# Eleven products of constant tiles per group on TensorE in the second layer of a graph network kernel

## The chip, the cores and the metric

One core of one Trainium2 chip. The metric is the device time of one execution in microseconds (us), the median of repeated runs.

## What is computed

Two graph layers over 3125 nodes with 256 features and 50000 edges, sorted by destination, each followed by a residual and a layer norm:

```python
x = layernorm(x + L0(x, edge_attr, src, dst, ...))   # edge MLP, gated, mean over the senders
x = layernorm(x + L1(x, [src, dst], edge_weight, W, a_src, a_dst))

def L1(x, edge_index, edge_weight, W, a_src, a_dst): # 4 heads of 64
    h = einsum('ni,hio->hno', x, W)
    e = (h@a_src)[:, src] + (h@a_dst)[:, dst]
    e = where(e >= 0, e, 0.2 * e) * edge_weight
    e_exp = exp(e - max(e))
    alpha = e_exp / (segment_sum(e_exp, dst)[:, dst] + 1e-10)
    return segment_sum(h[:, src] * alpha, dst)       # per head, heads side by side
```

The change is in the second layer, L1, in the part that scores and sums the edges.

## The kernel before

The 50000 edges lie in 391 blocks of 128, and 4 blocks make a group: 98 groups (NG). The first layer runs group by group to about 1640 us, then node products write the table HT (features and source score of each node), and from about 1700 us the second layer runs over the same 98 groups. The engines have instruction streams of their own, written out by hand and tied by semaphores. In the second layer's loop:

- POOL gathers the rows of HT by source index into Hg, one indirect DMA for each block (`gather_h_rows`, L1345). Hg is a ring of 12 groups (HGR): the gathers of group g wait for `s_xb`, which tells that DVE has used group g-12.
- DVE, in iteration i: `weighted_rows(i)` (xb, L911), `window_rows(i+1)` (in_window, L859), `edge_scores(i+1)` (L873 to L895, ends with `diag`, a diagonal matrix of the group's maxima), `one_hot(i+3)` (hot, L849), `carry_window(i-1)` (L928, L937, reads the sums of group i-1), `running_maximum(i+1)` (L902 reads `top_g` from the bank of `spread_maxima`, L906 makes neg_m).
- ACT, for group g: three exponentials of the scores with the running maximum (L1853, L1860, L1862); they wait for neg_m, and xb waits for them.
- PE, in iteration i: `destination_scores(i+2)` (L1601, 12 products of 4 columns into bank PAD), `spread_maxima(i+1)` (L1610, ones x diag, waits for diag), `window_sums(i)` (L1620, waits for in_window and xb).
- SP stores each group's sums and loads the destination remainders (`rem`) for two groups at a time.

So every group goes round one loop: top_g, neg_m (DVE), exponentials (ACT), xb, in_window, scores, diag (DVE), spread_maxima (PE), top_g of the next group (DVE). Scores of group g are in the first 16 columns of bank `PAD[g % 2]`, which is bank 0 or 1; columns 64 to 511 of the two banks are not read in this stage. `in_tile` (128 x 98 x 25, bf16) is a table that DVE makes once, before the loop; the constant "outside" of the semaphore `s_dc` is counted some instructions after it.

Of the kernel before, what the change touches and what calls it, by code (L numbers as in the profile page):

```python
# [6 lines left out]
P = 128  # L7
# [10 lines left out]
def build_program(nc, xT, x, src_cols, dst_cols, src_row, dst_row, eT, w_cols,  # L18
# [11 lines left out]
    NG = -(-NB // BLOCKS_PER_GROUP)  # L30
# [35 lines left out]
    def rows_of_block(b):  # L66
        return min(P, E - b * P)

    def blocks_of_group(g):
        return range(g * BLOCKS_PER_GROUP, min((g + 1) * BLOCKS_PER_GROUP, NB))  # L70
# [26 lines left out]
    with ctx:  # L97
        def sb(name, shape, dt=f32, scope=ctx):
            return scope.enter_context(nc.sbuf_tensor(name, shape, dt))

        def sem(name):
            return ctx.enter_context(nc.semaphore(name))
# [125 lines left out]
        outside = sb("outside", [1, 1], i32, sc)  # L228
        in_tile = sb("in_tile", [P, NG, NT], bf16, sc)
# [88 lines left out]
        PAD, PTOP, PS = bank[0:2], bank[2:4], bank[4:8]  # L318
# [10 lines left out]
        s_dc = sem("s_dc")  # L329
# [177 lines left out]
        def if_outside(eng):  # L507

            eng.wait_ge(s_dc, DC["outside"])
            return eng.If(eng.value_load(outside[0:1, 0:1], min_val=0, max_val=1))  # L510
# [4 lines left out]
        DC, B2 = {}, {}  # L515
# [895 lines left out]
        def _(pe):  # L1411
# [180 lines left out]
            def destination_scores(g):  # L1592

                pe.wait_ge(s_hot, g + 1)
                pe.wait_ge(s_adw, g // ADC + 1)
                if g >= 2:
                    pe.wait_ge(s_sc, 3 * (g - 2) + 1)
                for j, b in enumerate(blocks_of_group(g)):
                    n = rows_of_block(b)
                    for part in range(3):  # L1600
                        last = pe.matmul(PAD[g % 2][0:n, j * HEADS:(j + 1) * HEADS], hot[:, g % HOTR, j * P:j * P + n],  # L1601
                                         ad_p[:, part, g, :], start=part == 0, stop=part == 2)
                last.then_inc(s_ad, 1)

            def spread_maxima(g):

                pe.wait_ge(s_topc, 2 * g + 2)
                if g >= 2:
                    pe.wait_ge(s_mg, g - 1)
                pe.matmul(PTOP[g % 2][:, 0:P], ones[:, :], diag[:, g % 2, :], start=True, stop=True).then_inc(s_sp, 1)  # L1610

            def window_sums(g):

                pe.wait_ge(s_win, g + 1)
                pe.wait_ge(s_xb, g + 1)
                if g >= 4:
                    pe.wait_ge(s_carry, g - 3)
                for j, b in enumerate(blocks_of_group(g)):
                    n = rows_of_block(b)
                    last = pe.matmul(PS[g % 4][:, 0:BW], in_window[0:n, g % XBR, j, :], xb[0:n, g % XBR, j, :],  # L1620
                                     start=j == 0, stop=b == blocks_of_group(g)[-1])
                last.then_inc(s_S, 1)

            pe.wait_ge(s_hc, NT)
            pe.wait_ge(s_x1c, NT)
            for i in range(-2, NG):
                if i + 2 < NG:
                    destination_scores(i + 2)
                if 0 <= i + 1 < NG:
                    spread_maxima(i + 1)  # L1630
                if i >= 0:
                    window_sums(i)

            with if_outside(pe):
                pe.wait_ge(s_b2, B2["ones"])
# [21 lines left out]
                for t in range(NT):  # L1657
# [6 lines left out]
                    for k in range(DK):  # L1664
                        last = pe.matmul(bank[1][0:n, 0:OUT + 2 * HEADS], x1T_u[:, k, 0:n], Wc[:, k, :],
                                         start=k == 0, stop=k == DK - 1)
                    last.then_inc(s_vpe, 1)
                for b in range(NB):
                    n = rows_of_block(b)
                    pe.wait_ge(s_b2, B2[("weighed", b)])  # L1670
                    if b >= 1:
                        pe.wait_ge(s_vact, VACT1 + 1 + b)
                    pe.matmul(bank[0][0:n, 0:BW], in_window[0:n, 0, 0, 0:n], xb[0:n, 0, 0, :],
                              start=True, stop=True).then_inc(s_vpe, 1)
# [278 lines left out]
```

## Time and profile before

| | us |
|---|---|
| median of 3 runs | 2475.72 (2471.28 to 2481.22) |
| the profiled execution | 2482.71 |
| its span, first to last instruction | 2480.9 |
| second layer's group loop, first to last top_g | 1716.3 to 2412.2 |

The page gives for each engine the busy time and, in 40 slices of 62 us, its busy share and the clock granted to TensorE. The timeline lists instructions in order of time, equal ones merged with their count, and in brackets how long the engine had been idle and what released it. PE is the matmul side of TensorE, PEld its weight loads. A matmul's end is modelled, its start is recorded.

### The profile page before, as it was taken

Reading aid. Unit: us, or ns where it says so; the run is one execution under the profiler, and the core shown is the slowest. Engines: PE = TensorE matmul, PEld = TensorE weight load, DVE = VectorE, ACT = ScalarE, POOL = GpSimd, SP = SyncE. Lnnn points to the kernel's source line nnn. Section 1 sums busy time; section 2 is a strip of 40 time slices with the busy share of each in tenths; the row PEclk is TensorE's granted clock in tenths of the full one; section 3 lists DMA queues with packets and bytes.
Section 4 is the critical chain, followed back from the end, with each engine's and each line's share of the span. In section 5 each row is a group of like instructions: output and inputs, shape, how many; then the busy total and the mean of one; then the engine's idle time right before and its main releaser. Section 6 shows DMA issues by size and latency. Waiting matters only on the chain.

```text
span 2480.9 us, 41573 instructions
## 1 busy us (share of the span) xinstructions
PE 2001.8 (81%) x12990; PEld 1768.5 (71%) x12990; DVE 1594.5 (64%) x4240; ACT 1414.6 (57%) x2926; POOL 1467.6 (59%) x1204
## 2 busy tenths in 40 slices
PE   7699999999999999999999999944355555556560
PEld 6589999999999999899999999933244444444450
DVE  6466666666666666666666666652376656566575
ACT  4288888888888888888888888833011111111112
POOL 0327777877676677777777777424555565555503
PEclk9799999999999999999999999967566676766785
DMA  7678877777777777777777777564344444444413
GB/s 279 195 208 183 198 165 165 169 168 167 161 159 159 158 158 158 158 158 161 157 162 157 161 157 161 116 177 118 96 109 115 114 121 113 123 107 114 118 49 107
DMA packets 236177, 370.90 MB, mean 150 GB/s; under 512 B 35853, under 2 KB 168935, under 8 KB 235949
## 3 DMA queue, kind: packets, MB, share of 16 engines
q0 software_dynamic: 101232, 188.20, 38.4%
q1 hardware_dynamic: 134717, 179.94, 24.5%
q8 instruction: 108, 1.77, 0.3%
q14 instruction: 120, 0.98, 0.1%
HBM read 270.57 MB, written 97.45 MB: 148 GB/s over the span
## 4 chain that ended last, share of the span: by engine, by line
PE 56%; issue 17%; DVE 11%; another core or an unknown queue 5%; DMA 5%; ACT 4%; POOL 1%; SPq 0%; DVEq 0%; ACTq 0%; POOLq 0%
PE bank L1414 12%; PE bank L1415 12%; PE bank L1416 12%; PE bank L1466 4%; PE bank L1457 4%; PE bank L1483 3%; DMA accA<-ystage,to_a 2%; DVE in_window L859 2%; PE bank L1507 2%; PE bank L1518 2%; PE bank L1508 2%; PE bank L1519 2%; PE bank L1581 1%; ACT drop L1853 1%
## 5 line engine op out<-in xcount | busy, mean ns | idle before, releaser
L1310 POOL DMA_INDIRECT accA<-ystage,to_a x391 | 647.9, 1657 | 228.9 <-issue 107.7
L1316 POOL DMA_INDIRECT GA<-TA,src_c x391 | 424.0, 1084 | 334.4 <-issue 93.6
L1345 POOL DMA_INDIRECT Hg<-HT,src_c x391 | 371.5, 950 | 350.7 <-DVE xb L911 187.9
L1853 ACT ACTIVATE drop<-neg_m 128x1 f32<-128x1 f32 x98 | 28.9, 295 | 627.5 <-DVE neg_m L906 359.8
L1414 PE MATMUL bank<-h1h,W1h 128*128 128x512 f32 x882 | 349.6, 396 | 8.4 <-DVE h1l L531 7.6
L1416 PE MATMUL bank<-h1h,W1l 128*128 128x512 f32 x882 | 348.6, 395 | 0.0
L1415 PE MATMUL bank<-h1l,W1h 128*128 128x512 f32 x882 | 347.5, 394 | 0.0
L531 DVE TENSOR_TENSOR h2l<-h2f,h2h 128x512 fp32r<-128x512 f32 (+1 forms) x294 | 202.9, 690 | 203.2 <-ACT h2l L1689 72.2
L1610 PE MATMUL bank<-diag,ones 128*128 128x128 f32 x196 | 69.4, 452 | 304.5 <-DVE diag L895 249.9
L1620 PE MATMUL bank<-xb,in_window 128*128 128x260 f32 (+1 forms) x782 | 305.4, 561 | 0.0
L531 DVE TENSOR_TENSOR h1l<-h1f,h1h 128x512 fp32r<-128x512 f32 x294 | 195.1, 691 | 145.1 <-ACT h1h L1689 127.7
L1610 PEld LDWEIGHTS bank<-diag,ones 128*128 128x128 f32 x196 | 43.4, 276 | 313.5 <-DVE diag L895 255.5
L1620 PEld LDWEIGHTS bank<-xb,in_window 128*128 128x128 f32 (+1 forms) x782 | 220.2, 295 | 45.9
L1689 ACT ACTIVATE mh<-mf 128x512 fp32r<-128x512 f32 x196 | 124.0, 633 | 205.8 <-DVE mf L671 191.4
L1721 ACT ACTIVATE h1f<-bank 128x512 f32<-128x512 f32 (+1 forms) x392 | 206.9, 584 | 44.3 <-PE bank L1466 35.9
L1415 PE MATMUL bank<-W2l,h2h 128*128 128x256 f32 (+1 forms) x782 | 220.9, 282 | 0.0
L1414 PE MATMUL bank<-W2h,h2h 128*128 128x256 f32 (+1 forms) x782 | 219.8, 281 | 0.4 <-DVE mf L671 0.4
L1416 PE MATMUL bank<-W2h,h2l 128*128 128x256 f32 (+1 forms) x782 | 219.4, 281 | 0.0
L1746 ACT ACTIVATE h2f<-bank,b1c 128x512 f32<-128x512 f32 x294 | 201.9, 687 | 7.1 <-issue 1.7
L1414 PEld LDWEIGHTS bank<-h1h,W1h 128*128 128x128 f32 x882 | 166.7, 189 | 43.3 <-DVE h1l L531 9.8
L1416 PEld LDWEIGHTS bank<-h1h,W1l 128*128 128x128 f32 x882 | 166.1, 188 | 39.4
L1689 ACT ACTIVATE h2h<-h2f 128x512 fp32r<-128x512 f32 x294 | 185.5, 631 | 9.3
(208 smaller groups left out, 5189.7 us busy)
## 6 DMA issues: line engine op xcount, KB each, us to landing
TW<-TB SPq DMA_DIRECT2D x196, 203.0 KB
ef<-in_eT SPq DMA_DIRECT2D x97, 256.0 KB
bcast_i<-in_src_row SPq DMA_DIRECT2D x97, 256.0 KB
HB<-hist SPq DMA_DIRECT2D x98, 130.0 KB
rel<-RL SPq DMA_DIRECT2D x97, 128.0 KB
rem<-RD SPq DMA_DIRECT2D x48, 256.0 KB
TB<-stB SPq DMA_DIRECT2D x24, 406.0 KB, 3.3
accA<-zeros SPq DMA_DIRECT2D x4, 1677.0 KB, 13.5
```

Of the source, the lines that this page charges most:

```text
L531: return dve.tensor_tensor(o, full, hi.bitcast(f32), ALU.subtract)
L1310: return pool.indirect_dma_start(out=table, out_offset=bass.IndirectOffsetOnAxis(ap=rows, axis=0), in_=sums, in_offset=None, compute_op=AL ...
L1316: pool.indirect_dma_start(out=GA[0:n, b % (GAR * BLOCKS_PER_GROUP), :].bitcast(f32), out_offset=None, in_=TA, in_offset=bass.IndirectOffse ...
L1345: pool.indirect_dma_start(out=Hg[0:n, slot, :], out_offset=None, in_=HT, in_offset=bass.IndirectOffsetOnAxis(ap=src_c[0:n, b:b + 1], axis= ...
L1414: pe.matmul(o, lh, rh, start=first, stop=False)
L1415: pe.matmul(o, lh, rl, start=False, stop=False)
L1416: return pe.matmul(o, ll, rh, start=False, stop=last)
L1610: pe.matmul(PTOP[g % 2][:, 0:P], ones[:, :], diag[:, g % 2, :], start=True, stop=True).then_inc(s_sp, 1)
L1620: last = pe.matmul(PS[g % 4][:, 0:BW], in_window[0:n, g % XBR, j, :], xb[0:n, g % XBR, j, :], start=j == 0, stop=b == blocks_of_group(g)[-1])
L1689: return act.activation(o, i, ACT.Copy)
L1721: act.activation(h1f[0:k1(c), c, 0:n], PT[u % 2][0:k1(c), 0:n], ACT.Tanh).then_inc(s_tanh1, 1)
L1746: act.activation(h2f[:, m, 0:n], PL1[u % 2][:, 0:n], ACT.Tanh, bias=b1c[:, m:m + 1]).then_inc(s_tanh2, 1)
```

## The change

After the products of the sums of group i, PE issues eleven bf16 products: the first 128 columns of `in_tile` are the stationary tile, the next 448 the moving one, and the output goes to columns 64 to 511 of bank `PAD[(i + 1) % 2]`. Nothing reads the output, and no semaphore is raised. They are issued for i = 0 to 94, 95 x 11 = 1045 products. A wait of PE for "outside" stands ahead of the loop, so that `in_tile` is there.

```diff
+            def keep_running(g):
+
+                flat = in_tile[:, :, :].rearrange("p g t -> p (g t)")
+                for _ in range(11):
+                    pe.matmul(PAD[(g + 1) % 2][:, 64:512], flat[:, 0:P], flat[:, P:P + 448], start=True, stop=True)
+
             pe.wait_ge(s_hc, NT)
             pe.wait_ge(s_x1c, NT)
+            pe.wait_ge(s_dc, DC["outside"])
             for i in range(-2, NG):
                 if i + 2 < NG:
                     destination_scores(i + 2)
@@
                 if i >= 0:
                     window_sums(i)
+                if i + 3 < NG:
+                    keep_running(i)
```

## Rows read from the trace of the kernel before

**Rows 1.** The page's slices: PE's busy tenths, and its granted clock in tenths

```profile
PE   7699999999999999999999999944355555556560
...
PEclk9799999999999999999999999967566676766785
```

**Rows 2.** Stretches of the loop: busy time (count) of each engine, clock, DMA

```profile
1800.00:2350.00 550.00, 318.18 (x1759) 250.31 (x1760) 340.91 (x999) 54.60 (x237) 303.37 (x320) 0.68 0.46 116
2360.00:2400.00 40.00, 26.82 (x190) 21.53 (x189) 30.84 (x96) 5.53 (x24) 0.00 (x0) 0.82 0.15 46
```

**Rows 3.** Waits, 1800 to 2400 us: who waited for whom, total, times, longest

```profile
POOL Hg L1345 <- DVE xb L911: 173.3, 62, 7.7
DVE top_g L902 <- remote: 115.8, 36, 4.1
...
DVE top_g L902 <- issue: 7.7, 3, 3.3
```

**Rows 4.** Timeline, a group late in the loop, POOL's gathers over, clock high

```profile
2361.25 0.29 DVE L895 TENSOR_SCALAR diag<-ident,top_c 128x128 f32<-128x128 f32 x1
...
2361.59 0.49 PE L1610 MATMUL bank<-diag,ones 128*128 128x128 f32 x2 [0.48 <-DVE diag L895]
...
2362.48 0.28 DVE L902 TENSOR_REDUCE top_g<-bank 128x1 f32<-128x128 f32 x1
...
2363.67 0.44 PE L1601 MATMUL bank<-ad_p,hot 128*128 128x4 bf16 x12
...
2366.61 0.49 PE L1610 MATMUL bank<-diag,ones 128*128 128x128 f32 x2 [2.50 <-DVE diag L895]
...
2367.50 0.28 DVE L902 TENSOR_REDUCE top_g<-bank 128x1 f32<-128x128 f32 x1
```

**Rows 5.** Timeline of PE, the group before it, clock low

```profile
2356.57 0.79 PE L1610 MATMUL bank<-diag,ones 128*128 128x128 f32 x2 [6.40 <-DVE diag L895]
2357.15 3.67 PE L1620 MATMUL bank<-xb,in_window 128*128 128x260 f32 x8
2360.62 0.49 PE L1601 MATMUL bank<-ad_p,hot 128*128 128x4 bf16 x12
```

**Rows 6.** Timeline of a group with a stall, clock low in it

```profile
2029.24 0.80 PE L1610 MATMUL bank<-diag,ones 128*128 128x128 f32 x2 [0.46 <-issue]
2029.83 3.56 PE L1620 MATMUL bank<-xb,in_window 128*128 128x260 f32 x8
2031.58 0.95 POOL L1345 DMA_INDIRECT Hg<-HT,src_c  x1 [0.30 <-issue]
2034.25 0.29 DVE L902 TENSOR_REDUCE top_g<-bank 128x1 f32<-128x128 f32 x1 [4.04 <-remote]
2036.98 0.94 POOL L1345 DMA_INDIRECT Hg<-HT,src_c  x1 [4.45 <-DVE xb L911]
2038.39 0.79 PE L1610 MATMUL bank<-diag,ones 128*128 128x128 f32 x2 [4.71 <-DVE diag L895]
```

**Rows 7.** Timeline, the ends of three stalls with the clock high

```profile
2007.56 0.29 DVE L902 TENSOR_REDUCE top_g<-bank 128x1 f32<-128x128 f32 x1 [3.30 <-remote]
2019.06 0.95 POOL L1345 DMA_INDIRECT Hg<-HT,src_c  x1 [0.30 <-issue]
2020.08 0.29 DVE L902 TENSOR_REDUCE top_g<-bank 128x1 f32<-128x128 f32 x1 [2.39 <-issue]
2046.77 0.29 DVE L902 TENSOR_REDUCE top_g<-bank 128x1 f32<-128x128 f32 x1 [2.04 <-issue]
```

**Rows 8.** Stretches over stalls of 3.30, 2.39, 4.04 and 2.04 us: busy, clock, DMA

```profile
2003.30:2007.50 4.20, 2.51 (x22) 2.09 (x22) 0.74 (x3) 0.00 (x0) 2.67 (x3) 1.00 0.67 144
2016.60:2020.00 3.40, 2.52 (x22) 2.11 (x22) 0.88 (x4) 0.00 (x0) 2.79 (x3) 1.00 0.60 136
2029.20:2034.20 5.00, 4.44 (x22) 3.45 (x22) 0.80 (x3) 0.00 (x0) 2.72 (x3) 0.60 0.63 153
2043.40:2046.70 3.30, 2.52 (x22) 2.11 (x22) 0.77 (x3) 0.00 (x0) 2.68 (x3) 1.00 0.69 140
```

**Rows 9.** Timeline of PE in the first layer, products of 512 columns back to back

```profile
1002.75 0.39 PE L1415 MATMUL bank<-h1l,W1h 128*128 128x512 f32 x1
1002.98 0.40 PE L1416 MATMUL bank<-h1h,W1l 128*128 128x512 f32 x1
```

**Rows 10.** Groups of instructions: a bf16 weight load of 128 columns, 1800 to 2400

```profile
L1601 PEld LDWEIGHTS bank<-ad_p,hot 128*128 128x128 bf16 x1068 | 45.3, 103 | 24.7 <-issue 13.6
```

**Rows 11.** The constant "outside" on DVE, and PE's first products of the loop

```profile
L821 DVE TENSOR_SCALAR outside<-worst x1: 142/142/142, 1686.4 to 1686.4; 1x1 int32<-1x1 f32 x1
...
1708.10 0.78 PE L1601 MATMUL bank<-ad_p,hot 128*128 128x4 bf16 x24 [12.73 <-DVE hot L849]
```

## The prediction

> **What bounds the kernel now.** I read the slices of the page first. To slice 26, some 1640 us, PE is busy nine tenths or more at full clock; from there on it is busy about half the time and its clock stands at 0.5 to 0.8 [rows 1]. Over the loop's main part the mean clock is 0.68 and PE, DVE and POOL are each busy 55 to 62% [rows 2]: none is full, so the loop is bound by a chain of waits. The clock has two levels, 1.2 and 2.4 GHz, and 0.68 is a mix of them.
>
> The timeline shows the chain. Late in the loop, when POOL has no more gathers, top_g comes every 5.02 us (2362.48, 2367.50) [rows 4]. This pace doesn't depend on PE's clock: the group before it ran at the low clock (L1610 took 0.79 us instead of 0.49, the sums 3.67 us), and the same 5.02 us lie between its diag product and the next (2356.57, 2361.59) [rows 4, 5]. DVE and ACT set it, and the diag product is hidden behind DVE's hot and carry. So in a plain group a faster TensorE gives nothing.
>
> While POOL gathers, about every second group has a stall on top of it: DVE waits before top_g, with no releaser that the profile can name. The waits hold 36 stalls with 115.8 us and 3 with 7.7 us between 1800 and 2400, together 39 and 123.5 us, 3.17 us each [rows 3]. This is the only part of the loop in which I can see room. In the example the diag product is recorded at 2029.24 and top_g follows at 2034.25, after 5.01 us instead of 0.89 [rows 4, 6]. POOL's last gather before it ends at 2032.53, and POOL then idles 4.45 us until DVE's next xb frees the ring [rows 6]; the same wait sums to 173.3 us [rows 3]. So the ring is full, and POOL isn't late with data. What the stall is made of is the open question.
>
> **The change, part by part.** *The eleven products at the high clock.* The nearest row is the first layer's products of 512 columns, which start 0.23 us apart (1002.75, 1002.98) [rows 9]. For 448 columns that is 0.20 us, an estimate by columns, and 11 x 0.20 = 2.2 us per group. The bf16 weight loads take 103 ns each [rows 10] and fit under the product before. The trace has no bf16 product of this width. Its bounds are the same products taken at half their distance, 1.1 us for the eleven, and at the full 0.23 us of 512 columns, 2.5 us; I take 2.2, since the row differs from it in type alone once the columns are scaled. The Trainium skill ("TensorE: Matmul & The Clock Gate", Back-to-back issue gap) gives N/2.4 + 2.5 ns for a warm product, 189 ns for 448 columns; by it the eleven would take 2.08 us. Its rule for a cold array, N/1.2, would give 4.1 us.
>
> *Does it fit?* In a plain group at the high clock PE works from 2361.59 to 2364.11, 2.52 us, and is then idle 2.50 us, until the next diag [rows 4]. With 2.2 us more 0.3 us is left (0.1 to 0.5). What stands behind the new products in PE's queue is destination_scores(i+3), needed two groups later, and then spread_maxima(i+2), which the loop waits for. While the 0.3 us hold, the cost is nothing; the cover is DVE's and ACT's part of the 5.02 us. If it is gone, each us of excess is a us of the group.
>
> *At the low clock* the sums take 3.67 us instead of about half of it, and PE is busy from 2356.57 to 2361.11, 4.54 us of the 5.02 [rows 5]. Twice 2.2 us on top makes 8.9 us, 3.9 us too much. A loop that stayed at the low clock would cost 95 x 3.9 = 370 us, less what stalls absorb. I don't expect that, since a PE that is late has no idle time, and the first layer shows that a full PE keeps the high clock [rows 1]. Single low stretches are another matter (a rival, below).
>
> *The stalls.* In the stretches of three stalls at clock 1.00 the wait was 3.30, 2.39 and 2.04 us, on average 2.58; at 0.60 it was 4.04 [rows 6 to 8]. If the clock is held, I take 2.58 for all: 39 x (3.17 - 2.58) = 23 us less. The ends are 0 (the clock didn't cause it: the 3.30 speaks for that) and 39 x (3.17 - 2.04) = 44 us. I take the mean as three stretches are few and none of them is outlying.
>
> *The wait for "outside"* costs nothing: DVE has it at 1686.4, and PE's first product of the loop comes at 1708.10, released by DVE's hot [rows 11]. *The output columns* lie in the other bank than the one that DVE reads next for its scores, and raise no semaphore.
>
> The sum against the profiled execution: 2482.7 - 23, plus some 3 us for groups in which PE comes a little late (estimate: one group in ten late by 0.3 us), is 2463. The profiled execution lies 7 us above the median of the runs, so the forecast is 2475.7 - 20 = 2456 us.
>
> **The rivals.** *A. The clock is held and the stalls get shorter*, as summed: 2456 us (2435 to 2463).
>
> *B. The stall is not PE's.* In the example at high clock the last gather ends at 2020.01 and top_g starts at 2020.08; in that at low clock the distance is 1.7 us [rows 6, 7]. And the stalls are gone with the gathers [rows 4]. If what holds the semaphore is POOL's train of gathers, a held clock changes nothing: 2476 us (2465 to 2485). This also speaks against C, since a late PE would then hide in the stall.
>
> *C. PE comes too late, slower than before.* The stall leaves PE idle: with a work of 4.7 us per group and a distance of 9.15 us between two diag products (2029.24, 2038.39) [rows 6] some 4 us without work remain, and idle time is what the clock falls after now. If it falls once in each such pair of groups, the next group meets a stretch at half speed, and its new products cost up to 2.2 us more than the 0.3 us of room: 1.9 us, x 39 = 74 us, and 37 if half of it hides in the stall. That is 2513, up to 2550 us. It decides from where PE is late by more than 0.3 us in a plain group. The same holds if the eleven take over 2.5 us at the high clock.
>
> *D. The stalls go altogether*, because they come from the switching of the clock itself. 39 x 3.17 = 124 us less, 2352 us. The switching goes on in the late groups, without stalls [rows 4, 5]; this speaks against it.
>
> *E. The clock is not held at all*, since PE stays idle in the stalls, but nothing is late enough to matter: as B, no change.
>
> **How the numbers follow.** A 0.42, B with E 0.31, C 0.22, D 0.05. About 0.5%, 12 us, is what a measurement of this kernel can tell from no change. A lies mostly beyond it (0.38 of its 0.42 faster, 0.04 the same), D is faster; B is the same (0.27), with 0.02 on either side; C is slower. This makes faster 0.45, same 0.31, slower 0.24. The likeliest case is A, 2456, with its own range 2435 to 2463. The range of 8 in 10 leaves out D and the upper half of C: 2432 to 2512.
>
> **What would show it.** In the profile after, the mean clock of 1800 to 2350 us tells whether it is held (0.9 or more in A, under 0.8 in E). L1610 should take 0.49 us in nearly all groups. The spacing of the new products shows the 0.20 us, and PE's idle time before L1610 in plain groups the 0.3 us; if it is 0 and the releaser is no longer diag, C is at work, and the late groups' pace is over 5.02 us. The sum of the waits of top_g should fall from 123.5 us to about 100 in A and stay in B. The forecast is wrong if stalls at the high clock keep their 3.2 us, or if the clock still falls in them and PE is late behind them.

## The result

| | median of the runs, us | range | profiled execution | its span |
|---|---|---|---|---|
| before | 2476.72 | 2471.28 to 2481.22 | 2482.71 | 2480.9 |
| changed | 2518.11 | 2513.43 to 2524.58 | 2513.43 | 2511.6 |

The ratio is 1.0169, with a 95% interval of 1.0150 to 1.0188. The change makes the kernel 41 us slower; the forecast was 2456 us. The two profiled executions lie 31 us apart, since that of before is above its median and that of the change below; what the traces show accounts for these 31 us.

One thing has to be known for the numbers below. The same kernel before took 2458 to 2477 us in this comparison and three others, and 2280 us in two more. Each experiment has its own kernel before beside it, so the ratios stand; I call the first **comparisons with stalls** and the second **comparisons without stalls**, for that is what their traces differ in. Most of them ran on different chips (0 without stalls, 1 and 14 with them; for this first one no number is kept). But chip number 2 stands beside one of each sort, 2280 us and later 2472 us. So that the chip makes the difference is not shown.

### The profile page after: what moved, and what is told of

Same layout as the page of the kernel before. It is cut to its first block, busy times and chain, and to the rows that moved or that the text cites. A ratio compares the mean times of both kernels' runs of the same rounds, so it can differ in the third digit from the quotient of the medians.

```text
span 2511.6 us, 43707 instructions
## 1 busy us (share of the span) xinstructions
PE 2144.6 (85%) x14057; PEld 1818.7 (72%) x14057; DVE 1596.3 (64%) x4240; ACT 1416.2 (56%) x2926; POOL 1469.7 (59%) x1204
## 3 DMA queue, kind: packets, MB, share of 16 engines
q8 instruction: 117, 1.92, 0.3%
## 4 chain that ended last, share of the span: by engine, by line
PE 58%; issue 13%; another core or an unknown queue 10%; DVE 10%; ACT 4%; DMA 4%; SPq 1%; DVEq 0%; POOL 0%; ACTq 0%; POOLq 0%
PE bank L1415 13%; PE bank L1414 13%; PE bank L1416 13%; PE bank L1466 4%; PE bank L1457 4%; PE bank L1483 3%; PE bank L1507 2%; PE bank L1518 2%; PE bank L1508 2%; PE bank L1519 2%; DVE in_window L859 2%; ACT drop L1862 1%; PE bank L1581 1%; ACT xb L1871 1%
## 5 line engine op out<-in xcount | busy, mean ns | idle before, releaser
L1628 PE MATMUL bank<-in_tile 128*128 128x448 bf16 x1067 | 242.0, 377 | 20.0 <-issue 19.9
L1620 PE MATMUL bank<-xb,in_window 128*128 128x260 f32 (+1 forms) x782 | 243.0, 466 | 2.6 <-issue 2.6
L1628 PEld LDWEIGHTS bank<-in_tile 128*128 128x128 bf16 x1067 | 112.4, 105 | 137.0 <-issue 55.7
L1610 PE MATMUL bank<-diag,ones 128*128 128x128 f32 x196 | 54.5, 365 | 172.3 <-DVE diag L895 155.8
L1620 PEld LDWEIGHTS bank<-xb,in_window 128*128 128x128 f32 (+1 forms) x782 | 176.0, 236 | 33.7 <-issue 3.6
```

The lines of the kernel that those rows point to most:

```text
L1628: pe.matmul(PAD[(g + 1) % 2][:, 64:512], flat[:, 0:P], flat[:, P:P + 448], start=True, stop=True)
```

## The profile after

The slices of the page, PE's busy tenths and its granted clock, answer to [rows 1]:

```profile
PE   7599999999999999999999999852577777777780
...
PEclk9899999999999999999999999976788888888895
```

Stretches of the loop (busy time and count of PE, PEld, DVE, ACT, POOL, then clock, DMA share, GB/s) answer to [rows 2]:

```profile
1800.00:2350.00 550.00, 410.68 (x2487) 276.78 (x2486) 325.64 (x952) 52.54 (x228) 288.48 (x303) 0.86 0.44 110
2400.00:2440.00 40.00, 36.65 (x261) 25.23 (x259) 30.84 (x96) 5.54 (x24) 0.00 (x0) 1.00 0.15 40
```

So the change does what it says: the mean clock goes from 0.68 to 0.86, and to 1.00 in the late groups. DVE and POOL, though, do less in the same 550 us than before (DVE 952 instructions instead of 999). The waits of 1800 to 2400 us answer to [rows 3]:

```profile
POOL Hg L1345 <- DVE xb L911: 201.9, 72, 7.6
DVE top_g L902 <- remote: 151.1, 39, 4.2
...
DVE top_g L902 <- PE bank L1610: 0.7, 1, 0.7
```

There are as many stalls as before, 39, but they sum to 151.1 us and not to 123.5. The mean goes from 3.17 to 3.87 us. TensorE being late has one entry in this stretch, of 0.7 us. From the fourth top_g of the loop to the last it took 631 us before and 658 us after. Of these 27 us the stalls are 24 (151.1 less 123.5 is 28, but the window of the changed kernel takes in one stall that lies ahead of it before; taken stall by stall over the same groups it is 147.1 less 123.5). The rest of the 31 us between the two spans is the start of the loop, 4 us.

A late group of the changed kernel (start, duration, engine, line, in brackets the idle time before) answers to [rows 4]:

```profile
2402.73 0.49 PE L1610 MATMUL bank<-diag,ones 128*128 128x128 f32 x2 [0.42 <-DVE diag L895]
...
2403.63 0.28 DVE L902 TENSOR_REDUCE top_g<-bank 128x1 f32<-128x128 f32 x1
...
2404.82 2.24 PE L1628 MATMUL bank<-in_tile 128*128 128x448 bf16 x11
2406.90 0.44 PE L1601 MATMUL bank<-ad_p,hot 128*128 128x4 bf16 x12
2407.76 0.49 PE L1610 MATMUL bank<-diag,ones 128*128 128x128 f32 x2 [0.42 <-DVE diag L895]
...
2408.65 0.28 DVE L902 TENSOR_REDUCE top_g<-bank 128x1 f32<-128x128 f32 x1
```

The pace is 5.02 us, as before. The eleven products take 2404.82 to 2406.90, 2.08 us, and PE is still idle for 0.42 us before the diag product. And a stall of the changed kernel, answering to [rows 6, 7]:

```profile
2007.09 0.95 POOL L1345 DMA_INDIRECT Hg<-HT,src_c  x1 [0.31 <-issue]
...
2007.18 0.47 PE L1610 MATMUL bank<-diag,ones 128*128 128x128 f32 x2
...
2009.24 2.24 PE L1628 MATMUL bank<-in_tile 128*128 128x448 bf16 x11
2009.63 0.29 DVE L902 TENSOR_REDUCE top_g<-bank 128x1 f32<-128x128 f32 x1 [3.92 <-remote]
...
2012.37 0.95 POOL L1345 DMA_INDIRECT Hg<-HT,src_c  x1 [4.33 <-DVE xb L911]
```

The diag product is recorded at 2007.18 at the high clock, its modelled end is 2007.65, and top_g comes 1.98 us behind that; in the plain group above it comes 0.41 us behind it. POOL's last gather ends at 2008.04 and top_g starts at 2009.63, 1.59 us behind it. In the kernel before this distance falls into three classes of 13 stalls each: 0.05 to 0.32 us (2020.01 to 2020.08 in [rows 7]), 0.73 to 1.01 us, and 1.51 to 1.78 us (2032.53 to 2034.25 in [rows 6]). In the changed kernel all 38 stalls from the seventh group on are of the last kind, 1.49 us and more. That is the slowdown; what does it was the question for the runs.

The trace also holds the times of the semaphore updates, which the timeline doesn't print. In 36 of the 39 stalls of the kernel before (for the other three no update is recorded) the update that tells of the diag product is recorded 2.5 to 4.5 us behind the product's modelled end, and top_g starts 0.02 us behind the update. In the changed kernel it is so in all 38 (2.0 to 4.9 us). In the groups without a stall, from the seventh on, the update comes 0.01 us behind the end (0.14 at most). So top_g starts as soon as it is told; what is late is TensorE's word. Whether the product itself or only its update is held up can't be seen, as the ends of matmuls are modelled.

A correction to the text ahead: the products are issued for i = -2 and -1 too, since the condition is only i + 3 < NG. There are 97 x 11 = 1067 of them, not 1045. Grouped by line, after:

```profile
L1628 PE MATMUL bank<-in_tile 128*128 128x448 bf16 x1067 | 242.0, 377 | 20.0 <-issue 19.9
```

## Experiments

**Theories.** T1: a stall is made by POOL. While gathers go out without a gap, the semaphore of TensorE that top_g waits for comes through late; the change lengthens the end of that. T2: the stall is TensorE's (its clock, its array time). C, a rival of the prediction: TensorE is late by itself, at the low clock.

### Half of the gathers (first in a comparison without stalls)

```diff
                 for b in blocks_of_group(g):
-                    gather_h_rows(b, ...)
+                    if g < HGR or b % BLOCKS_PER_GROUP < 2:
+                        gather_h_rows(b, ...)
```

From the 13th group on, two of the four gathers of each group are left out; the wait of DVE for the landings counts accordingly.

> The kernel before, but from the thirteenth group on POOL gathers only the first two blocks of each group (the other two blocks of xb are made of the rows that stand in the ring from earlier groups), so POOL needs 2.5 us of a group instead of 5.0. Theory 1 (a train of gathers without a pause holds PE's semaphores back until it ends; that is the stall before top_g): the stalls go, the loop runs at 5.02 us per group, some 39 x 3.2 = 124 us less, about 2350 us. Theory 2 (the stalls come from TensorE, its clock or its order of work): the stalls stay, 2460 to 2480 us.

> The same half of the gathers left out, in the changed kernel with its eleven products per group. Theory 1: no stalls, and PE has 0.3 us of room per group, so the products cost nothing: the same time as half_gathers within 5 us. Theory 2 (PE comes late after stretches at the low clock and this is what the 41 us are): some part of them stays, 10 to 40 us over half_gathers.

Here the kernel before took 2280.15 us. half_gathers: 2280.44 us, ratio 0.9997 (0.9987 to 1.0007). half_gathers_eleven: 2291.72 us, 1.0055 (1.0038 to 1.0072). Nothing could be removed because nothing was there: the traces have no stall in either kernel, so neither theory was tested. But something else costs 11 us, which the first expectation (within 5 us) had not. A repetition came out without stalls again:

> The kernel before with half of the gathers left out from the thirteenth group on (their blocks are made of older rows), again. Without stalls on this chip: 2280 us, as before. With them: theory 1 says that they go, about 2350 us; theory 2 that they stay, 2460 to 2480 us.

2279.9 us, 1.0000 (0.9990 to 1.0011).

### Five products, and narrow ones (comparison without stalls)

```diff
-                for _ in range(11):
+                for _ in range(5):
```

> The changed kernel with five products instead of eleven (1.0 us instead of 2.2 us per group at the high clock). Theory 1a (the longer stalls follow PE's work or its clock): the stalls are between the two kernels, 3.2 to 3.9 us, 2485 to 2505 us. Theory 1b (any product issued behind the sums does it): 2513 to 2520 us, as with eleven. Theory 2 (lateness): PE is never late with five, 2470 to 2480 us.

2284.14 us, ratio 1.0017 (1.0007 to 1.0027).

```diff
-                    pe.matmul(PAD[(g + 1) % 2][:, 64:512], flat[:, 0:P], flat[:, P:P + 448], ...)
+                    pe.matmul(PAD[(g + 1) % 2][:, 64:128], flat[:, 0:P], flat[:, P:P + 64], ...)
```

> The changed kernel with eleven products of 64 columns instead of 448: the same number of instructions, 0.3 to 0.7 us of work per group. If the number of instructions makes the stalls longer: 2513 to 2520 us, stalls of 3.9 us. If it is the time that TensorE works, or its clock: 2472 to 2482 us, stalls of 3.2 us as before.

2280.71 us, 1.0004 (0.9994 to 1.0014). Both expectations were written for stalls, and none of their numbers could be met. Without stalls the cost goes with array time: narrow products cost nothing, five some 4 us, eleven 10 to 12 (next).

### Both kernels again, unchanged (comparison without stalls)

> The kernel before, for its profile on the chip of the experiments: 2280 us without a stall before top_g, top_g every 5.02 us, all 391 gathers of POOL without a wait; or, where the chip has the stalls, 2476 us and the profile of before.

> The changed kernel itself, on the chip of the experiments. On the chip of the four runs before, where the kernel before takes 2280 us and five products added 4 us, no stalls stand before top_g. Theory 1 (stalls there, and only there, the change costs much): about 2291 us, as half of the gathers with eleven products. If the 41 us came from PE's lateness alone, they show here too: 2320 us. On a chip on which the kernel before takes 2476 us: 2518 us.

The kernel before: 2281.61 us, 1.0004 (0.9993 to 1.0014). The changed one: 2292.61 us, 1.0045 (1.0029 to 1.0062), 10 us by the ratio and 12 by the medians. The timeline of the kernel before here, a stretch in the middle of the loop:

```profile
2000.91 0.96 POOL L1345 DMA_INDIRECT Hg<-HT,src_c  x1 [0.30 <-issue]
2001.66 0.28 DVE L902 TENSOR_REDUCE top_g<-bank 128x1 f32<-128x128 f32 x1
...
2005.93 0.96 POOL L1345 DMA_INDIRECT Hg<-HT,src_c  x1 [0.30 <-issue]
2006.68 0.28 DVE L902 TENSOR_REDUCE top_g<-bank 128x1 f32<-128x128 f32 x1
```

POOL gathers all the time, without catching up with the ring, and top_g still comes every 5.02 us and never waits. So POOL's gathers alone don't make a stall; it takes something more, which differs between the comparisons. All 92 updates of the diag products from the seventh group on come 0.01 us behind the modelled end here. What the 10 to 12 us are is seen in the changed kernel's waits (whole execution) and one of the places:

```profile
DVE top_g L902 <- PE bank L1610: 12.3, 10, 2.4
```

```profile
1729.14 0.80 PE L1610 MATMUL bank<-diag,ones 128*128 128x128 f32 x2 [3.60 <-DVE diag L895]
1729.73 3.67 PE L1620 MATMUL bank<-xb,in_window 128*128 128x260 f32 x8
...
1733.19 3.09 PE L1628 MATMUL bank<-in_tile 128*128 128x448 bf16 x11
1733.77 0.29 DVE L895 TENSOR_SCALAR diag<-ident,top_c 128x128 f32<-128x128 f32 x1
1736.12 0.44 PE L1601 MATMUL bank<-ad_p,hot 128*128 128x4 bf16 x12
1736.42 0.47 PE L1610 MATMUL bank<-diag,ones 128*128 128x128 f32 x2
...
1736.92 0.29 DVE L902 TENSOR_REDUCE top_g<-bank 128x1 f32<-128x128 f32 x1 [1.91 <-PE bank L1610]
```

PE was idle for 3.60 us (DVE had a long step in that group), the clock is low in the sums (3.67 us instead of 1.92), the new products start late and run at the low clock at first, and the diag product starts only 2.36 us after DVE has finished diag (1734.06, 1736.42). This group took 6.95 us. It is the mechanism of C, at ten places: the first groups and those behind DVE's long steps. The kernel before has 1.5 us of such waits in three places.

### No products behind pauses (comparisons with stalls)

```diff
-                if i + 3 < NG:
+                if 0 <= i < NG - 3 and i % ADC != 3 and i != ADC // 2 + 1:
                     keep_running(i)
```

> The changed kernel without its eleven products at the places where the trace of it shows top_g waiting for the diag product: before the first group (they are issued for two iterations of the prologue too) and in the group behind each of DVE's long steps (window_scores, last_rows), where TensorE has just stood idle and its clock is low. Theory C (the 12 us that the change costs on this chip are PE coming late at the low clock, 10 waits with 12.3 us together): they go, 2279 to 2284 us. Rival (each group loses a little, 0.13 us x 95): still about 2290 us.

> The eleven products, but none for i below 0, for the iterations in which DVE has its long step (i = 3, 17, 31, ...) and for i = 8: the places behind which TensorE was found late at the low clock. Without stalls (before at 2280 us): if the 12 us of the change are the late groups behind those steps (C), they go: 2281 to 2284 us; if they are spread over all groups, 11 of 12 us stay: 2291 us. With stalls present the lengthening of the stalls stays and only some 10 of the change's 41 us go: 2485 to 2495 us.

Both labels are one kernel, and both came out in comparisons with stalls (before 2458.46 and 2469.36 us). skip: 2494.98 us, 1.0149 (1.0117 to 1.0180); skip2: 2499.60 us, 1.0122 (1.0105 to 1.0139). That is some 5 to 12 us less than the change costs, in the direction expected, and most of the cost stays; the interval of skip overlaps that of the change. The share of late-ending stalls stays too (32 of 35, 31 of 34), and what got less is the number of stalls, 34 or 35 instead of 38. So this doesn't prove C where there are stalls. Without stalls C rests on the waits above; skip didn't run there.

### More products, more DMAs (comparison with stalls)

> The changed kernel with fourteen products instead of eleven, 0.56 us more per group at the high clock (0.188 us each in the trace after the change). The trace shows PE idle 0.48 us before the diag product with eleven. If all of this is room, the excess is 0.1 us per group and the time 2300 to 2315 us (the late groups cost more too). If 0.28 us of it is what the wait itself takes, the excess is 0.36 us per group: 2325 to 2340 us.

2514.74 us against 2458.46, 1.0224 (1.0193 to 1.0256). Both times expected were for a comparison without stalls. What they were to tell is seen in the last groups of this trace: the fourteen take 2.65 us (2402.96 to 2405.61), PE has no idle time left before the diag product, and top_g still comes every 5.03 us. So all of the idle time was room.

The next two have six small DMAs of SP in each group, and nothing else changed in the first:

```diff
+                    for k in range(EXTRA):            # EXTRA = 6, 128 x 8 bytes each
+                        c = g * EXTRA + k
+                        sp.dma_start(extra[:, c, :], x[0:P, c * 2 % D:c * 2 % D + 2]).then_inc(s_extra, 16)
```

> The kernel before with six more DMAs per group, issued by SP behind the store of the group's sums: 128 rows of 8 bytes each into a tile that nothing reads, 96 more semaphore updates per group beside the 128 or so of the gathers, the store and the remainders. A try to bring about the stalls that the chip of the first comparison shows. Theory S (there the path of the semaphore updates is full): the stalls before top_g come back in part, over 2290 us. Otherwise 2278 to 2286 us, as the data is small.

> The changed kernel with the same six additional DMAs per group. Theory S: stalls as in the run of the kernel before with these DMAs, and longer ones with the products, more than 12 us above it. Otherwise 12 us above it, as without them.

updates: 2503.66 us, 1.0181 (1.0140 to 1.0222). updates_eleven: 2517.86 us, 1.0239 (1.0198 to 1.0279), each from two executions. The stalls were there without the DMAs, so the runs don't tell whether these DMAs can bring them about. But without a single product the stalls end late in 35 of 39 cases and sum to 143.6 us. With the products on top only 14 us are added. Alone the DMAs cost 45 us and the products 41; together they cost 59. (The 41 are of the first comparison; fourteen products, beside the same kernel before as these, cost 56.) Two causes that don't add up share an effect that saturates, and fourteen products, with stalls of 3.8 us as with eleven, say so too.

### Half of the gathers again (comparison with stalls)

> The kernel before with only two of the four gathers of each group from the 13th group on (it leaves out gathers; the rows that they would bring are those of an earlier group). If the kernel before takes some 2460 us in this comparison, its loop has the stalls, and: if they come from POOL's gathers going out without a gap (T1), POOL's pause of 2.5 us in each group lets the held semaphore through early, and nearly all of 38 x 3.2 = 123 us go: 2330 to 2350 us. If the stalls are TensorE's or the table's (its clock, the DMAs of rem), nothing changes: 2455 to 2470 us. If the kernel before takes 2280 us, there are no stalls to remove and both theories say no change (2280 us).

2346.75 us against 2469.36, ratio 0.9502 (0.9484 to 0.9520). The time is what T1 expected. From the fourth top_g on no stall is left; in 1800 to 2400 top_g has no entry among the waits at all. From the middle of the loop:

```profile
2000.15 0.94 POOL L1345 DMA_INDIRECT Hg<-HT,src_c  x1 [2.84 <-DVE xb L911]
2001.40 0.95 POOL L1345 DMA_INDIRECT Hg<-HT,src_c  x1 [0.30 <-issue]
2002.45 0.28 DVE L902 TENSOR_REDUCE top_g<-bank 128x1 f32<-128x128 f32 x1
...
2005.17 0.94 POOL L1345 DMA_INDIRECT Hg<-HT,src_c  x1 [2.83 <-DVE xb L911]
2006.42 0.94 POOL L1345 DMA_INDIRECT Hg<-HT,src_c  x1 [0.30 <-issue]
2007.47 0.28 DVE L902 TENSOR_REDUCE top_g<-bank 128x1 f32<-128x128 f32 x1
```

The clock here is 0.74 between 1800 and 2350 us, and 0.77 up to 2270 us, near the end of this loop, where the kernel before has 0.68; that is far from held, and no stall is left. So all 123 us of stalls hang on POOL's gathers, and not on TensorE's clock. This kills T2 for the stalls of the kernel before. It doesn't tell what of the gathers it is: with POOL's instructions their DMAs went too (116 GB/s in the loop before, 98 in 1800 to 2250 us here). POOL's trains of gathers are also seen in the start of the kernel before, where the ring of 12 groups is filled by one row of 56 gathers. Its waits from 1700 to 1780 us, and top_g:

```profile
DVE top_g L902 <- issue: 23.8, 1, 23.8
PE bank L1610 <- issue: 23.6, 1, 23.6
PE bank L1601 <- issue: 18.7, 9, 3.3
```

```profile
1716.31 0.29 DVE L902 TENSOR_REDUCE top_g<-bank 128x1 f32<-128x128 f32 x1 [5.00 <-remote]
...
1745.81 0.29 DVE L902 TENSOR_REDUCE top_g<-bank 128x1 f32<-128x128 f32 x1 [23.81 <-issue]
...
1776.05 0.29 DVE L902 TENSOR_REDUCE top_g<-bank 128x1 f32<-128x128 f32 x1 [7.36 <-remote]
```

Two groups take 60 us. PE stands as well, with nothing to wait for that the trace shows.

### Narrow and five products again (comparison with stalls)

> Eleven products of 64 columns instead of 448: as many instructions of TensorE as the change, a seventh of its columns; the clock is not held. With stalls present (before at some 2460 us): if the number of TensorE's instructions lengthens the stalls (each has to be taken in by the same path that the semaphore updates use), they are 3.9 us as with the eleven, +0.7 x 38 = 27 us, 2490 us. If it is the time or the clock of the array, they stay at 3.2 us and the time at 2460 us (2455 to 2470). Without stalls (before at 2280 us) both say 2280 us.

2514.12 us against 2469.36, ratio 1.0180 (1.0163 to 1.0197). Its stretch of the loop, its wait and a stall:

```profile
1800.00:2350.00 550.00, 308.47 (x2475) 246.89 (x2474) 322.74 (x943) 52.31 (x228) 286.02 (x301) 0.73 0.43 110
```

```profile
DVE top_g L902 <- remote: 156.0, 40, 4.2
```

```profile
2006.04 0.49 PE L1610 MATMUL bank<-diag,ones 128*128 128x128 f32 x2
...
2008.12 0.42 PE L1628 MATMUL bank<-in_tile 128*128 128x64 bf16 x9
...
2009.35 0.22 PE L1628 MATMUL bank<-in_tile 128*128 128x64 bf16 x2 [0.81 <-issue]
2010.08 0.20 PE L1601 MATMUL bank<-ad_p,hot 128*128 128x4 bf16 x2 [0.51 <-issue]
2010.78 0.41 PE L1601 MATMUL bank<-ad_p,hot 128*128 128x4 bf16 x10 [0.51 <-issue]
2010.91 0.29 DVE L902 TENSOR_REDUCE top_g<-bank 128x1 f32<-128x128 f32 x1 [3.90 <-remote]
```

The products take a seventh of the columns and leave the clock at 0.73, and the stalls are 3.9 us, all 39 of them ending late. So neither array time nor clock lengthens them, it is that there are more instructions. The stalls are as long as the first expectation says; its time, 2490 us, is not met. And TensorE, whose products should follow each other without a break, gets stuck three times in the stall, for 0.5 to 0.8 us with no releaser.

> Five products of 448 columns. With stalls present: if what lengthens them is that the clock is held, so that all stalls end in the same late way (1.6 us behind POOL's last gather), five do it as eleven and fourteen did: stalls of 3.9 us, 2490 us, less the part that comes from a late TensorE. If it grows with the number of products, 11 us of the 25: 2472 us. Without stalls: 2284 us, the late groups gone but for 4 us.

2508.44 us, 1.0158 (1.0139 to 1.0177), 38 of 39 stalls late, 3.85 us each. Five do nearly as much as eleven, as the first of the two expectations says (its 2490 us is missed by 18); but its reason, the clock, has fallen with narrow2.

### One product, and activations instead (comparison with stalls)

> The change with one product of 448 columns per group instead of eleven. With stalls present: if the lengthening needs a number of instructions between the sums and the destination scores, one is too few, 2465 us (stalls of 3.2 to 3.4 us); if already the wait for 'outside' ahead of the loop or a single product tips all stalls into the late class, 2500 us. Without stalls both say 2280 us.

2487.85 us against 2471.83, 1.0065 (1.0048 to 1.0082), between the two expectations.

```diff
                 last.then_inc(s_ex, 1)
+                for k in range(8):
+                    act.activation(spare[:, g * 8 + k:g * 8 + k + 1], ident[:, 0:1], ACT.Exp)
```

> The kernel before with eight one-column activations per group on ScalarE, behind its exponentials, and nothing on TensorE. With stalls present: if what lengthens the stalls is any further instruction, on whatever engine (instructions or their semaphore traffic on a shared path), the stalls are 3.9 us, 2490 to 2510 us, as with the six small DMAs of SP and the products. If it takes instructions of TensorE between the sums and the destination scores, the time stays at 2455 to 2475 us. Without stalls both say 2280 us.

2482.44 us, 1.0039 (1.0025 to 1.0052): a little slower, between the two expectations. The kernels in order of the share of their stalls that end late, over 1.25 us behind POOL's last gather (worked out from each trace; a stall is a wait of top_g of over 1.7 us, behind the seventh top_g of the loop; breath is the next experiment):

| kernel | late stalls | sum of the stalls, us | ratio |
|---|---|---|---|
| before | 13 of 39 | 123.5 | 1 |
| act8 | 18 of 38 | 123.7 | 1.0039 |
| one | 20 of 38 | 128.4 | 1.0065 |
| updates | 35 of 39 | 143.6 | 1.0181 |
| breath | 23 of 24 | 100.8 | 0.9975 |
| five2 | 38 of 39 | 150.1 | 1.0158 |
| fourteen | 39 of 40 | 152.0 | 1.0224 |
| changed | 38 of 38 | 147.1 | 1.0169 |
| updates_eleven | 38 of 38 | 150.2 | 1.0239 |
| narrow2 | 39 of 39 | 152.0 | 1.0180 |

One product does a little, five do nearly all. Fourteen add nothing: changed, fourteen, narrow2 and updates_eleven all take 2514 to 2518 us; their ratios differ because the kernel before took 2458 us in one comparison and 2477 in another. The stalls of before were traced in the first comparison alone, so they are to be held against spans and not against the ratios: the span of narrow2 is 33 us over the traced 2480.9 us, with 28.5 us more in stalls, and that of act8 1 us over it, with as much in stalls as before. That act8 does anything to the stalls is therefore not shown.

### A short gap for POOL (comparison with stalls)

```diff
                     gather_h_rows(b, b % (HGR * BLOCKS_PER_GROUP), s_hg[g % HGR])
+                if g >= 1:
+                    pool.wait_ge(s_breath, g)
+                pool.iota(breath[:, :], pattern=[[1, 512]], base=0, channel_multiplier=0).then_inc(s_breath, 1)
```

> The kernel before with one iota of 512 columns on POOL after the four gathers of each group: nothing is left out, and the row of gathers has a gap once per group (some 0.6 us, an estimate from the 0.23 us that an iota of 128 columns takes in the trace of before). With stalls present (before at some 2460 us): if a short gap is enough to let the held semaphores through, the stalls end with the group's gathers at the latest; the groups take 5.6 to 6.0 us instead of 6.5 on average, 40 to 80 us less, 2390 to 2420 us. If only a long gap (2.5 us and more) lets them through, the stalls stay and the iotas lengthen the trains: 60 us more at the most, 2470 to 2520 us. Without stalls (before at 2280 us): POOL gets longer than DVE's 5.02 us and sets the pace with some 5.7 us per group: 2280 + 30 to 60 us.

2463.97 us against 2471.83, ratio 0.9975 (0.9963 to 0.9988). It is faster than both kernels, by 8 us instead of the 40 to 80 hoped for. Its waits of 1800 to 2400 us and a stretch:

```profile
POOL Hg L1347 <- DVE xb L913: 107.7, 29, 5.7
DVE top_g L904 <- remote: 100.8, 24, 4.8
...
DVE top_g L904 <- PE bank L1615: 7.2, 18, 1.2
```

```profile
2002.49 0.58 POOL L1360 IOTA breath<- 128x512 int32 x1
2003.23 0.95 POOL L1347 DMA_INDIRECT Hg<-HT,src_c  x1 [0.16 <-issue]
...
2005.52 0.29 DVE L904 TENSOR_REDUCE top_g<-bank 128x1 f32<-128x128 f32 x1 [0.31 <-PE bank L1615]
```

This gap (1.68 us from gather to gather instead of 1.25, filled with the iota) doesn't end the stalls. It lets two groups through between them instead of one: 24 stalls of 4.2 us replace 39 of 3.2. 23 of the 24 end late, without a further instruction of TensorE or a DMA of SP. Whether a gap in which POOL stands idle would do more stays open: a version in which POOL waits behind its four gathers for three of them to land gave no time. Without stalls it wasn't run either; there POOL would need 5.43 us per group (three distances of 1.25 us and one of 1.68, an estimate) and be slower than DVE's 5.02, so I expect it to lose.

## Why the prediction was wrong, step by step

- **Plain groups** at 5.02 us, whatever the clock: right, in both kernels and with stalls or without.
- **Eleven products, 2.2 us, room 0.3 us**: 2.08 and 0.42 us, and fourteen show that all of the idle time is room. Right; the price by the Trainium skill ("TensorE: Matmul & The Clock Gate", Back-to-back issue gap), 189 ns each or 2.08 us, is met to the hundredth.
- **The clock is held**: nearly, 0.86 in the loop, under the 0.9 that I had named for it, and 1.00 in the late groups.
- **Groups in which PE comes late, 3 us** (an estimate): 0.9 us in two waits of top_g in the changed kernel. Without stalls the term was too small: 12.3 us against 1.5 before.
- **"Outside" costs nothing**: right; PE's first product of the loop comes at 1708.66 us, again behind DVE's hot.
- **The stalls at 2.58 us with the clock held**: this step failed. The term priced them by the clock; they follow the end of POOL's gathers. They are 3.87 us each, nearly as many as before, so that instead of 23 us less there are 24 us more. The step took three stretches at clock 1.00 [rows 7, 8] against one at 0.60 [rows 6]. Over all 39 stalls of the same trace, the 20 whose diag product ran at the high clock have a mean of 2.89 us. Even that small relation was no cause: narrow2 leaves the clock at 0.73 and has stalls of 3.9 us, half_gathers3 leaves it at 0.74 and has none. The bounds that I gave for this term, 0 and 44 us less, excluded a loss without a reason; the loss is what came.
- **Rival B** had where the stall comes from: top_g follows the end of POOL's gathers, and half_gathers3, with half of them left out, has none of the 123 us. Its conclusion, no change, was wrong: what hangs on POOL's gathers can still be made longer by instructions elsewhere.
- **Rival C** gave the sign and, with 2513 us, nearly the time, by luck: its mechanism isn't at work where its 37 us were put, as in the trace with stalls PE is late once in 600 us. Without stalls it is real and costs 10 to 12 us, behind DVE's long steps and at the start, not behind stalls. The test named for it told the two apart: PE's idle time before L1610 in a plain group is 0.42 us and not 0, and its releaser is still diag.
- **D** and **E**: the stalls didn't go, and the clock was held.
- The range, up to 2512 us, missed 2518 by 6 us.

**What stays open.** Shown is that the stalls need POOL's full number of gathers and something that only some comparisons have, that the update of TensorE's semaphore is recorded late in them (before and changed), that they end 0.1, 0.9 or 1.6 us behind the last gather, and that further instructions of TensorE or DMAs of SP turn the early endings into late ones. Not shown is the path that they share. That TensorE's own products get stuck for 0.5 to 0.8 us in the stall speaks for something behind TensorE that its instructions or their semaphore increments have to pass.

One rival is untested: the recording. The traces with stalls have lost semaphore updates. The kernel before has 25990 of them recorded with stalls and 40390 without, though it is the same program, and the thirteen traces with stalls or beside them have 25280 to 29664, the seven without 37679 to 40390. The loss begins in the first layer (1052 against 1596 updates between 100 and 200 us). More instructions and more DMAs are also more to record. Against it speaks that half_gathers3 has the loss (26404 updates) and no stall, and that act8, with eight more instructions of ScalarE in each group, has stalls that sum to no more than before. The stalls and the loss may still have one cause, or the recording may make the stalls; every execution here has its span and clock recorded, and none shows the time without that.

## What to carry to other kernels

Before a wait is priced by what correlates with it, find who must stop for it to end, and read all its cases: here the end of each stall followed another engine's last instruction. Look at the recorded update of the semaphore too: here it told that DVE started 0.02 us after it, and that TensorE's word was late. Filler work on an engine that isn't the bottleneck is not free even where its array time fits into idle time, since instructions themselves can lengthen waits elsewhere; and a higher clock buys nothing where the pace is set by other engines. If one kernel can take 8% more in one comparison than in another, repeat a surprising result beside its own kernel before, and try the cause where the effect is seen.

## What the hardware showed that I had not expected

- The same kernel takes 2280 us in some comparisons and 2458 to 2477 in others. The difference lies in this loop: 123 us in 39 stalls, and most of the rest at its start, where two groups took 60 us (1716.31 to 1776.05).
- An indirect gather of 128 rows occupies POOL for 0.95 us, every 1.25 us. In the kernel before, in a comparison with stalls, eight of them on end went with updates of TensorE's semaphore recorded 2.5 to 4.5 us late, and 56 on end with a wait of top_g of 24 us.
- Eleven products of 64 columns, 0.8 us of TensorE or less, end at the same time as eleven or fourteen of 448: 2514.12, 2518.11 and 2514.74 us.
